# A DLRM tower on one core: pair products emptied by two instructions per tile, and a first layer contracted 27 partitions at a time in four row quarters

## What is computed

```python
e = jnp.stack([tbl_0[ids[:, 0]], ..., tbl_26[ids[:, 26]]], axis=1)   # (512, 27, 128)
dot = jnp.einsum('bnd,bmd->bnm', e, e)
z = dot.reshape(512, 27 * 27)[:, idx]                                 # the 351 pairs i < j
h = jnp.concatenate([z, dense_ctx], axis=1)                           # 367
h = jnp.maximum(h @ W_top1 + b_top1, 0.0)                             # 512
h = jnp.maximum(h @ W_top2 + b_top2, 0.0)                             # 256
y = h @ W_top3                                                        # 1
```

## Time and profile before

| | us |
|---|---|
| median of three runs | 204.6 |
| lowest and highest run | 203.13, 206.66 |
| span of the profiled execution | 200.6 |
| TensorE busy, matmuls | 127.1 |
| VectorE busy | 117.1 |
| ScalarE busy | 86.6 |
| GpSimd busy | 74.4 |
| moved from HBM | 13.37 MB |

### The profile page before, as it was taken

One profiled execution on the slowest core, in us unless ns is written; L12 is line 12 of the kernel. 1 busy time (PEld: TensorE's weight loads), 2 busy tenths in 40 slices (PEclk: granted clock), 3 DMA queues, 4 the chain that ended last, 5 costly groups with the idle time before them and its releaser, 6 DMA issues.

```text
span 200.6 us, 2216 instructions
## 1 busy us (share of the span) xinstructions
PE 127.1 (63%) x677; PEld 109.7 (55%) x677; DVE 117.1 (58%) x360; ACT 86.6 (43%) x307; POOL 74.4 (37%) x78
## 2 busy tenths in 40 slices
PE   7539509820409999501955889585696749759094
PEld 3117307610207888401944789484696649759094
DVE  0057045310319996122299999999999950599901
ACT  2112022092004845004397469866676903754411
POOL 5777787877726877773553000000000000000000
PEclk9955976995555999955695559999788888966969
DMA  4855448944445741221110000000000000000000
GB/s 75 154 166 167 161 160 228 235 157 167 156 147 111 154 133 54 52 52 26 44 52 13 13 0 0 5 0 2 0 3 0 0 2 0 3 0 0 0 0 0
DMA packets 6396, 13.51 MB, mean 67 GB/s; under 512 B 2321, under 2 KB 3086, under 8 KB 6385
## 3 DMA queue, kind: packets, MB, share of 16 engines
q1 hardware_dynamic: 4048, 8.59, 13.0%
q0 software_dynamic: 2336, 4.79, 11.4%
HBM read 13.37 MB, written 0.00 MB: 67 GB/s over the span
## 4 chain that ended last, share of the span: by engine, by line
DVE 35%; PE 16%; issue 15%; SPq 10%; DMA 10%; ACT 6%; another core or an unknown queue 6%; ACTq 0%; DVEq 0%
DVE G L484 25%; PE ps L339 8%; PE ps L363 6%; DMA raw<-in_tbl 5%; DVE G L491 5%; DMA csb<-in_consts 4%; SPq L257 4%; DVE onehot L436 3%; ACT G L551 2%; ACT eT L537 2%; DVE lo L423 2%; SPq L242 1%; PE ps L380 1%; ACT eT L543 1%
## 5 line engine op out<-in xcount | busy, mean ns | idle before, releaser
L275 POOL DMA_INDIRECT E<-in_tbl,ids_sb x73 | 73.7, 1010 | 35.1 <-issue 20.7
L484 DVE COPY_PREDICATED G<-mask,ps 32x24 f32<-32x24 int32 (+1 forms) x240 | 63.4, 264 | 14.9 <-ACT G L551 10.3
L339 PE MATMUL ps<-eT 128*128 128x108 f32 x256 | 41.6, 332 | 29.7 <-DVE G L491 14.3
L551 ACT COPY G<-ps 32x24 f32<-32x24 f32 (+1 forms) x240 | 47.4, 198 | 26.2 <-PE ps L339 23.0
L339 PEld LDWEIGHTS ps<-eT 128*128 128x128 f32 x256 | 39.0, 241 | 32.4 <-issue 15.2
L298 PE MATMUL ps<-onehot,hi 125*128 125x512 f32 (+1 forms) x72 | 33.8, 469 | 30.9 <-issue 26.4
L436 DVE TENSOR_SCALAR onehot<-idsb,csb 125x1024 fp32r<-125x1024 int32 (+1 forms) x40 | 26.1, 696 | 39.0 <-remote 26.5
L298 PEld LDWEIGHTS ps<-onehot,hi 125*128 125x128 f32 x72 | 16.0, 222 | 37.8 <-issue 34.3
L300 PE MATMUL ps<-onehot,lo 125*128 125x512 f32 (+1 forms) x72 | 31.8, 441 | 0.0
L510 ACT CAST hi<-raw 125x1024 fp32r<-125x1024 f32 (+1 forms) x11 | 9.8, 890 | 39.1 <-DMA raw<-in_tbl 25.8
L423 DVE TENSOR_TENSOR lo<-raw,hi 125x1024 fp32r<-125x1024 f32 (+1 forms) x11 | 11.3, 1023 | 12.9 <-issue 10.8
(11 more groups left out here) (25 smaller groups left out, 30.5 us busy)
## 6 DMA issues: line engine op xcount, KB each, us to landing
raw<-in_tbl SPq DMA_DIRECT2D x7, 500.0 KB
idsb<-in_ids_hot SPq DMA_DIRECT2D x4, 500.0 KB
E<-in_tbl,ids_sb POOLq DMA_INDIRECT x73
raw<-in_tbl SPq DMA_DIRECT2D x4, 250.0 KB
w_sb<-in_w SPq DMA_DIRECT2D x1, 768.0 KB
w_sb<-in_w SPq DMA_DIRECT2D x1, 512.0 KB
w1d<-in_w_dense SPq DMA_DIRECT2D x1, 256.0 KB
idsb<-in_ids_hot SPq DMA_DIRECT2D x1, 187.5 KB
```

The costliest lines, as they stand in the source:

```text
L275: pool.indirect_dma_start(out=E[:, t % 2, slot, :], out_offset=None, in_=tables[f], in_offset=bass.IndirectOffsetOnAxis(ap=ids_sb[:, t * F ...
L339: mm = pe.matmul(ps[:, window_bank(t, w) + g // 4, at:at + 4 * F], eT[:, c0:c0 + 4, :].rearrange("p s f -> p (s f)"), eT[:, c0:c0 + 4, 0:F ...
L484: op = dve.copy_predicated(G[32 * m:32 * m + 32, t, :, cols], mask[32 * m:32 * m + 32, 0:KT].unsqueeze(2).to_broadcast([32, KT, ng]), src)
L551: op = act.copy(G[32 * m:32 * m + 32, a, :, cols], src)
```

## The change

The hot stage keeps its form. It has 11 tables instead of nine, all for all tiles, in six pairs (the last with one), so 16 features are gathered per tile; `E` holds three tiles. The host lays the hot tables out in 128 partitions (`hot_rows`, the last three zero) and the ids as 16-bit integers. The constants are loaded by ScalarE's queue.

The products are made per sample: 32 weight columns (27 features and the first five of what follows), 27 moved ones, with the result in one of four groups of 32 PSUM partitions. A tile's 128 results fill two banks. Features 0 to 25 form a ring: column k of `Z` holds for each feature i its product with feature k or with feature k+13, by which of them follows it in the ring; the fourteenth column holds the product with the last feature. Both come from the same partition, so a tile is emptied by one ScalarE copy of 14 columns by 32 samples and one masked VectorE copy of 13 columns. Tile t's samples stand in columns 32t to 32t+31 of `Z`, in all four partition groups.

The first layer is made for half a batch at a time (`PARTS = 2`): for each of four blocks of 128 outputs, 14 columns of `Z` and one of `D` (dense numbers and a row of ones for the bias), each in four matmuls that contract 27 (or 17) partitions of one quarter into a bank of its own. The weights are therefore laid out four times, 15x512 numbers per partition. Layers 2 and 3 are made for 256 samples at a time, in 8 and 4 matmuls.

```diff
-        eT = sb("eT", [P, B, SLOTS])
-        G = sb("G", [P, T, KT, P])
-        w1_sb = sb("w1_sb", [P, KT, H1])
+        eT = sb("eT", [P, T, P * F + SLOTS - F])
+        Z = sb("Z", [P, COLS, P])
+        w1_sb = sb("w1_sb", [P, COLS + 1, H1])
...
+        TURN, DOTS, L1, L2, L3 = 2, 4, (0, 1, 6, 7), 0, 1
+        def left(first, n):
+            return ps[:, DOTS:DOTS + 2, 0:GB * F].rearrange("p b (g j) -> p j b g", j=F)[:, first:first + n, :, :]
+        def place(t, n):
+            return Z[:, 0:n, 32 * t:32 * t + 32].rearrange("p k (b g) -> p k b g", b=2)
...
+            sp.dma_start(ids_sb[:, :], ids).then_inc(ids_in, 16)
+            sp.dma_start(raw[:, 0, :], hot_rows[:, 0, :]).then_inc(raw_in[0], 16)
...
+                for k in PAIRS[b]:
+                    if k >= RAWS:
+                        sp.wait_ge(lo_done, k - RAWS + 1)
+                    sp.dma_start(raw[:, k % RAWS, :], hot_rows[:, k, :]).then_inc(raw_in[k], 16)
+                if b == 2:
+                    sp.dma_start(D[:, :], dense).then_inc(dense_in, 16)
+                    sp.dma_start(w1_sb[:, :, :], w1).then_inc(w_in, 16)
...
-                for g in range(WG[t][w]):
-                    c0 = t * P + 4 * (sum(WG[t][:w]) + g)
-                    at = (g % 4) * PITCH
-                    mm = pe.matmul(ps[:, window_bank(t, w) + g // 4, at:at + 4 * F],
-                                   eT[:, c0:c0 + 4, :].rearrange("p s f -> p (s f)"),
-                                   eT[:, c0:c0 + 4, 0:F], start=True, stop=True)
+                for g in range(GB):
+                    for s in range(4):
+                        c = (32 * s + GB * half + g) * F
+                        mm = pe.matmul(ps[32 * s:32 * s + 32, DOTS + half, g * F:(g + 1) * F],
+                                       eT[:, t, c:c + SLOTS], eT[:, t, c:c + F], start=True, stop=True)
...
+                for n in range(N1):
+                    for k in range(COLS + 1):
+                        for s in range(4):
+                            rows = slice(32 * s, 32 * s + (F if k < COLS else DENSE + 1))
+                            x = Z[rows, k, NP * u:NP * (u + 1)] if k < COLS else D[rows, NP * u:NP * (u + 1)]
+                            mm = pe.matmul(ps[:, L1[s], n * NP:(n + 1) * NP], w1_sb[rows, k, n * P:(n + 1) * P], x,
+                                           start=(n == 0 and k == 0), stop=(k == COLS), skip_group_check=True)
...
+            for t in range(T):
+                dve.wait_ge(base_out, t + 1)
+                dve.copy_predicated(place(t, HALF), mask[:, :].unsqueeze(2).unsqueeze(3)
+                                    .to_broadcast([P, HALF, 2, GB]), left(0, HALF)).then_inc(dots_out, 1)
...
+                elif kind == "dots" and b == 1:
+                    act.wait_ge(dots_done, 2 * (a + 1))
+                    act.copy(place(a, COLS), left(HALF, COLS)).then_inc(base_out, 1)
...
+                    for s in range(4):
+                        act.activation(h1[:, :, s, :], ps[:, L1[s], 0:N1 * NP].rearrange("p (n b) -> p n b", n=N1),
+                                       ACT.Relu).then_inc(l1_out, 1)
```

More of the change, by code:

```diff
@@ L74 @@
 I32 = mybir.dt.int32
+I16 = mybir.dt.int16
 U32 = mybir.dt.uint32
@@ L77 @@
 ACT = mybir.ActivationFunctionType
[L80 to L109, removed]
@@ L112, in outputs @@
-def outputs(t):
-    last = max(b for b, (_, s0, s1) in enumerate(BATCHES) if s0 <= t * P < s1)
-    return sum(len(x[0]) for x in BATCHES[:last + 1])
-STEPS = """
[L123 to L129, removed]
+STEPS = """
+    hot 0 0, hot 0 1, turn 0 0, hot 1 0, hot 1 1, turn 0 1, hot 2 0, turn 0 2, hot 2 1, turn 0 3,
+    hot 3 0, turn 1 0, hot 3 1, turn 1 1, hot 4 0, hot 4 1, turn 1 2, hot 5 0, hot 5 1,
+    dots 0 0, dots 0 1, turn 1 3, dots 1 0, dots 1 1, l1 0, turn 2 0, l2 0, l3 0, turn 2 1,
+    turn 2 2, turn 2 3, dots 2 0, dots 2 1, turn 3 0, turn 3 1, turn 3 2, turn 3 3,
+    dots 3 0, dots 3 1, l1 1, l2 1, l3 1"""
@@ L130, with build @@
 STEPS = [(x.split()[0], *map(int, x.split()[1:])) for x in STEPS.split(",")]
-def build(nc, ids, ids_hot, dense, tables, w1, w1_dense, b1, w2, b2, w3, consts, take_c, out):
-    turns = [x[1:] for x in STEPS if x[0] == "turn"]
-    dots = [x[1:] for x in STEPS if x[0] == "dots"]
+TURNS = [x[1:] for x in STEPS if x[0] == "turn"]
+def build(nc, ids, ids_hot, hot_rows, tables, dense, w1, w2, wb, consts, take_c, out):
     with ExitStack() as ctx:
@@ new lines, in layer1, with layer2 @@
+                mm.then_inc(l1_done, 1)
+            def layer2(u):
+                pe.wait_ge(l1_out, 4 * (u + 1))
+                for n in range(N2):
+                    for k in range(N1):
+                        mm = pe.matmul(ps[:, L2, n * 4 * NP:(n + 1) * 4 * NP], w2_sb[:, k, n * P:(n + 1) * P],
+                                       h1[:, k, :, :].rearrange("p s b -> p (s b)"), start=(n == 0 and k == 0),
+                                       stop=(k == N1 - 1), skip_group_check=True)
+                mm.then_inc(l2_done, 1)
@@ L393, in layer3 @@
+            def layer3(u):
+                pe.wait_ge(l2_out, u + 1)
+                for v in range(2):
+                    for k in range(N2):
+                        mm = pe.matmul(ps[:, L3, v:v + 1], h2[:, k, v * P:(v + 1) * P],
+                                       wb_sb[:, N2 + k:N2 + k + 1], start=(v == 0 and k == 0), stop=(k == N2 - 1),
+                                       skip_group_check=True)
                 mm.then_inc(l3_done, 1)
@@ L397, in _ @@
             for _ in range(WARM):
-                pe.matmul(ps[:, MLP, :], warm[:, 0:P], warm[:, :], start=True, stop=True)
+                pe.matmul(ps[:, 7, :], warm[:, 0:P], warm[:, :], start=True, stop=True)
             pe.wait_ge(const_in, 16)
@@ L494, in _ @@
[L494 to L501 removed]
+                    if b == 0 and c < len(PAIRS[0]):
+                        low(PAIRS[0][c])
@@ new lines, in column_mask @@
+def column_mask():
+    mask = np.zeros((4, 32, HALF), np.int32)
+    for k in range(HALF):
+        mask[:, k + 1:k + HALF + 1, k] = 1
+    return mask.reshape(P, HALF)
+def first_layer_rows():
+    rows = np.full((32, COLS), -1)
+    for k in range(HALF):
+        for i in range(RING):
+            if i != k:
+                j = k if k + 1 <= i <= k + HALF else k + HALF
+                a, b = sorted((ORDER[i], ORDER[j]))
+                rows[i, k] = b * (b - 1) // 2 + a
+    for i in range(RING):
+        a, b = sorted((ORDER[i], ORDER[RING]))
+        rows[i, HALF] = b * (b - 1) // 2 + a
@@ L634 @@
     }
-    for f in range(F):
+    for f in GAT_F:
         arrays[f"tbl_{f}"] = inputs[f"tbl_{f}"]
```

500 lines of the change are left out of this document (152 added, 348 removed).

## The result

The changed kernel takes 218.97 us (median of four runs, 217.26 to 220.09), the kernel before 204.67 beside it; the ratio is 1.072, with an interval of 1.063 to 1.081. It is slower, as forecast, and 13 us quicker than the 232 us that were predicted. But the time is not lost where the prediction put it.

A forecast was written before the change was run, and what follows sets the result against it. It took the hot stage as bound by no engine (waits) and the product stage by VectorE. Hot stage 76, products 57.3, first layer 65.3 and rest 30.7 gave 229 us, plus 3 for the median: 232, range 203 to 285.

The forecast's parts named there:

- first layer: First layer after the products: 960 pairs of weight load and matmul at 68 ns each, 65.3 us in all.
- the rest: Behind the hot stage: evictions 12.2, emptyings and later layers 14.2, uncovered turns 2.0, store 2.3 us; 30.7 us in all.
- The gathers cost nothing: Hot stage and after: 64 gathers at 1.33 us end at 88 us, the last needed only past 150 us.
- the 76 us for the hot stage: Hot stage: products start at 76 us instead of 94.4, with bounds of 61 and 94 us.
- rival C: Hot stage stays at 94 us because the change removes no cause of its unnamed waits: 250 us; chance 0.14.
- The padding: Hot-stage loads over 128 partitions instead of 125: all loads at 233 GB/s less the gathers' 52, so 181.
- the price of a small pair: Product stage: one weight load and its matmul cost 56 ns, between 28 and 112; 1024 pairs, 57.3 us.
- rival D: Products and first layer: instruction issue sets 112 ns per pair everywhere, 355 us; chance 0.03.
- Rival A: First layer: the four row quarters don't load at once, 136 ns a pair, 298 us (274 at full clock); chance 0.17.
- The masked copy: Product stage: VectorE's one masked copy per tile, 416 elements, takes 2.0 us as upper bound, 0.6 as lower.
- Layer 2: Second layer, twice per half: 16 pairs at 0.22 us, twice the small pair for twice its columns, 3.5 us.
- Rival B: Products and first layer: small pairs follow their columns, 28 ns each, 61 us instead of 123, giving 171 us; chance 0.12.

## Why the prediction was right, and where it was wrong

**The sign and the range held by luck, through errors that cancelled.** Against the predicted span of 229 us: products 35 less, first layer 14 less, the rest 2 more, the hot stage 34 more; together 13 less.

**"The gathers cost nothing" failed, and with it the 76 us for the hot stage.** The step asked only when each gather's data is needed, and not what issuing does to TensorE. In the trace of before the wait stood open, 26.5 us "remote" and 26.4 "issue"; the prediction called it unnamed, and let it vanish in its middle and stay in rival C. It neither vanished nor stayed, it grew (34.0 us), because the third `E` tile removed GpSimd's pauses (17.7 us of the time go with that tile). Without gathers the first product comes at 62.3 us, next to the lower bound of 61.

**The padding was right and undersized.** It was put at 181 GB/s beside the gathers for want of a row. Ahead of the weights the loads came at 304 less the gathers' some 50, and without gathers 327 GB/s were moved from 10 to 20 us.
**Products: the price of a small pair was too high by four to five.** 56 ns were chosen between 28 and 112; alone a pair is 30, with column groups alternating 10 to 15, below the lower bound, which had not allowed for column groups overlapping. The gaps make it some 21 ns per pair over a whole tile, 2.6 times less than chosen. The Trainium skill ("TensorE: Matmul & The Clock Gate", Back-to-back issue gap) has about 62 ns per matmul with hardware decode off, the case for rival D; 10 ns a pair rule that out here.

**First layer: right for half a wrong reason.** 68 ns were the middle of 28 and 112 over a clock of 0.82. The rows show the lower bound, 28 (as measured at a clock of 1.00), over the granted 0.50 to 0.51: 53. Rival A is out. The Trainium skill ("TensorE: Matmul & The Clock Gate", Measured speedup vs the span model) has 3.07x for four row quarters; these rows, 213 to 53, have 4.0x.

**Rest.** The masked copy is 0.62 us, not 2.0, and ScalarE's 0.53, not 1.0: a slope read from copies of 24 and 36 elements doesn't carry to 416. Layer 2 took 5.4 and 6.1 us where 3.5 stood. The two errors nearly cancel, 32.6 us instead of 30.7. **Rival B** (171 us) meets the kernel without gathers only in the number: there the products and the layer are 73 us and not 61, and the hot stage is 62 and not 76.

## What to carry to other kernels

A stretch of "remote" or "issue" waits that ends 1 to 8 us behind GpSimd's last gather is to be suspected of the gathers; compare when a matmul ended with when its signal was acted on, and ask of each change whether it lets GpSimd run longer without a pause. Give GpSimd short pauses, have gathers out before the products start, and load tables over 128 partitions. Where weights are loaded for each small matmul, move as many columns as fit.

## What was not expected of the hardware

- Beside back-to-back gathers the signal of a finished matmul reached the other engines up to 36 us late (59.2 to 95.0). Matmuls that wait for nothing were issued more slowly, down from 5 pairs per 0.74 us to one per 2.8 us after some 30 us. For the hot stage a pause of 0.97 us in every 6 heals it. The slowness outlasts the last gather, by 1 us with such pauses (101.9 to 102.9), by 5 us behind 64 gathers in a row (89.8 to 95.0) and by 7.5 behind 48 of them beside the products (123.0 to 130.5). The mechanism inside is open, and so is why the kernel before took 189 us in one set and 203 to 205 in the others.
- The granted clock was 0.50 throughout a first layer with 64 moved columns, TensorE busy all the time (25.87 of 25.90 us), and rose to 1.00 within 5.4 us in the same layer with 128.
- 16-bit ids did not speed up the one-hot compare: 763 ns for 1024 columns, 762 before.
